# GNN and MoE layer: the gathered table of normed rows as plain fp32 instead of three bf16 parts

## The reference

```
xn  = layernorm(x)
agg = segment_sum(xn[src], dst) / max(degree, 1)
z   = concat([xn, agg]) @ gnn_weight            # 512 x 256
x1  = x + z / norm(z) + gnn_bias
xl  = layernorm(x1)
expert, gate = argmax and max of softmax(xl @ gate_w + gate_b)   # 8 experts
y   = w2[e] @ relu(w1[e] @ xl + b1[e]) + b2[e]  # 256 -> 1024 -> 256, capacity 977 a expert
out = x1 + y * gate                             # dropped tokens: y is of weight 0
```

## Time and profile before

| | us |
|---|---|
| median of 3 runs | 1463.89 (1462.98 to 1465.42) |
| the profiled execution | 1461.04, its span 1459.3 |
| mean granted TensorE clock | 0.94 |

### The profile page before, as it was taken

How to read it: one execution, slowest core, us unless ns; L and a number is a source line. 1 busy time by engine, 2 the same in 40 slices (tenths; PEclk the granted TensorE clock), 3 DMA queues, 4 the chain that set the end, 5 groups by cost and what they waited for, 6 DMA issues and landing times.

```text
span 1459.3 us, 33188 instructions
## 1 busy us (share of the span) xinstructions
PE 1101.7 (75%) x6813; PEld 797.5 (55%) x6814; DVE 874.6 (60%) x3786; ACT 495.6 (34%) x1397; POOL 923.8 (63%) x946
## 2 busy tenths in 40 slices
PE   0105667668888888888889889888888888876885
PEld 0004445446666666666666666666666666654553
DVE  2973545446666676666667666666756675654443
ACT  1651111223333333333333333333333333343442
POOL 3446676757777777777777777777776777600101
PEclk9998777879999999999999999999999999998998
DMA  7257888865565656566565655656564656411111
GB/s 210 89 185 211 299 267 287 286 213 162 163 179 165 183 162 186 168 174 179 155 176 149 181 159 168 168 160 174 149 179 131 176 152 174 127 38 43 37 48 35
DMA packets 126952, 238.78 MB, mean 164 GB/s; under 512 B 21453, under 2 KB 85250, under 8 KB 126932
## 3 DMA queue, kind: packets, MB, share of 16 engines
q0 software_dynamic: 55904, 160.90, 38.6%
q1 hardware_dynamic: 71028, 77.69, 16.9%
HBM read 207.46 MB, written 39.29 MB: 169 GB/s over the span
## 4 chain that ended last, share of the span: by engine, by line
DVE 25%; DVEq 20%; PE 20%; issue 17%; DMA 14%; ACT 3%; SPq 1%; ACTq 1%; POOL 1%; POOLq 0%
PE ps_q L726 7%; DVEq L1300 5%; PE ps_h L793 4%; DMA ring<-parts_d,idx 4%; PE ps_a L784 4%; DVE sel L1049 3%; DVEq L1120 3%; DMA b_b<-in_L_ffn_b 2%; DMA parts_d<-w_sb 2%; DVEq L903 2%; DVE row L1163 2%; DMA out<-ys,node_i 2%; DMA w_sb<-in_x 2%; DVE row L1167 1%; DVE acc L1058 1%
## 5 line engine op out<-in xcount | busy, mean ns | idle before, releaser
L476 POOL DMA_INDIRECT ring<-parts_d,idx x784 | 768.2, 980 | 278.5 <-issue 184.4
L726 PE MATMUL ps_q<-ring,sel 128*128 128x256 bf16 x2928 | 474.6, 287 | 165.8 <-DVE sel L1049 90.4
L726 PEld LDWEIGHTS ps_q<-ring,sel 128*128 128x128 bf16 x2928 | 255.1, 102 | 325.0 <-issue 205.4
L1049 DVE SCALAR_TENSOR_TENSOR sel<-lane,block,dst_t 128x512 bf16<-128x512 bf16 x245 | 184.1, 751 | 121.2 <-PE ps_q L732 63.2
L812 PE MATMUL ps_b<-w_sb,hid_t 128*128 x864 | 231.0, 397 | 23.7 <-ACT hid_t L646 23.7
L793 PE MATMUL ps_h<-w_sb,hid_t 128*128 x432 | 211.1, 615 | 5.7 <-ACT hid_t L625 5.7
L1058 DVE TENSOR_TENSOR acc<-acc,ps_q 128x257 f32 x245 | 103.2, 421 | 164.0 <-ACT cat L600 68.1
L812 PEld LDWEIGHTS ps_b<-w_sb,hid_t 128*128 128x128 f32 x864 | 150.1, 190 | 48.3 <-issue 33.7
L732 PE MATMUL ps_q<-ones_bf,sel 128*128 128x1 bf16 x976 | 167.3, 171 | 0.0
L784 PE MATMUL ps_a<-gw_sb,cat_t 128*128 128x256 f32 x416 | 127.6, 435 | 0.9 <-ACT cat_t L622 0.9
L646 ACT ACTIVATE hid_t<-ps_t,b_t 128x128 f32<-128x128 f32 x432 | 117.6, 383 | 30.5 <-PE ps_t L801 30.5
(11 more groups left out here) (189 smaller groups left out, 1307.2 us busy)
## 6 DMA issues: line engine op xcount, KB each, us to landing
w_sb<-in_L_ffn_w SPq DMA_DIRECT2D x32, 512.0 KB
ring<-parts_d,idx POOLq DMA_INDIRECT x784
disp_d<-ys SPq DMA_DIRECT2D x8, 1040.0 KB, 12.9
parts_d<-w_sb SPq DMA_DIRECT2D x6, 1344.0 KB, 5.1
xs<-disp_d SPq DMA_DIRECT2D x55, 130.0 KB, 3.2
ys<-disp_d SPq DMA_DIRECT2D x55, 130.0 KB
b_b<-in_L_ffn_b SPq DMA_DIRECT2D x55, 128.0 KB
xb<-in_x SPq DMA_DIRECT2D x51, 128.0 KB
```

What stands on the lines that cost most here:

```text
L476: pool.indirect_dma_start(ring[:, (k % 2) * TQ + j, :], None, parts_d[:, :], bass.IndirectOffsetOnAxis(ap=idx[:, k * TQ + j:k * TQ + j + 1 ...
L726: mm = pe.matmul(ps[:, 0:D], sel[:, s, j, :], ring[:, (k % 2) * TQ + j, part * D:(part + 1) * D], start=(j == 0 and part == 0), stop=(j == ...
L1049: dve.scalar_tensor_tensor(out=sel[:, s, :, :], in0=lane[:, :].rearrange("p (j m) -> p j m", j=1).to_broadcast((P, TQ, P)), scalar=block0[ ...
```

## The change

The table in HBM is `xn_d`, one fp32 row of 256 a node (1024 bytes). x has room for all seven groups in w1's memory; it is normalised in place, six of seven blocks on ACT and one on DVE, and each group is stored when both are done. The parts, their copies and their slots are gone. The statistics of two groups share one reciprocal step, with EPS added in it. The ring holds 257 fp32 a slot, the last of them 1, written once by POOL; the selection is fp32. A tile is one fp32 matmul of 257 columns, the last tile of a visit one of 256 and one of a single column. The first x group comes in two pieces. The second half of the edge lists is loaded as 96 rows by SP and one by POOL, the last x and table rows as 96 and 10. DVE clears `acc` in one instruction at the start, ahead of its statistics, and takes the edge reductions between the first two groups (by a minimum on the four results instead of a masked copy of the list). ACT's copies of the transposed edge lists come before its first group, into and out of two PSUM tiles in turn. The filler of the dispatch buffer comes from `hid`, not `ys`, so the first chunk loads are issued before trip 0; ACT waits for the fills before trip 8. w2 is loaded together with w1 at the start of a trip. POOL clears only the tail of the last group and makes the identity earlier.

```diff
@@ -25,9 +25,10 @@
 FULLQ = E_EDGES // QE
 TAIL = E_EDGES - FULLQ * QE
 PAD_DST = 16383
-NPART = 3
 XG = 7
-XA = 5
+XA = 6
+LASTA = LAST // 16 * 16
+ROWSA = (FULLQ - QH) // 16 * 16
 NG = NB // XG
...
-    parts_d = nc.dram_tensor("parts_d", (N, NPART * D), BF16, kind="Internal").ap()
+    xn_d = nc.dram_tensor("xn_d", (N, D), FP32, kind="Internal").ap()
...
-        ring = sb("ring", [P, 2 * TQ, NPART * D], BF16)
+        ring = sb("ring", [P, 2 * TQ, AW], FP32)
...
-        sel = sb("sel", [P, 2, TQ, P], BF16)
+        sel = sb("sel", [P, 2, TQ, P], FP32)
...
+            def store_xn(g):
+                blocks = XG if g < NG - 1 else XG - 1
+                sp.dma_start(xn_d[ds(g * (XG * P), blocks * P), :].rearrange("(b p) d -> p b d", p=P),
+                             xin[g][:, 0:blocks * D].rearrange("p (b d) -> p b d", d=D)).then_inc(xn_out, 16)
+                if g == NG - 1:
+                    for lo, hi in ((0, LASTA), (LASTA, LAST)):
+                        sp.dma_start(xn_d[(NB - 1) * P + lo:(NB - 1) * P + hi, :],
+                                     xin[g][lo:hi, (XG - 1) * D:XG * D]).then_inc(xn_out, 16)
 
...
-                sp.dma_start(staged[0:FULLQ - QH, QE:2 * QE],
-                             dram[QH * QE:FULLQ * QE].rearrange("(p e) -> p e", e=QE)).then_inc(stage_in, 16)
+                sp.dma_start(staged[0:ROWSA, QE:2 * QE],
+                             dram[QH * QE:(QH + ROWSA) * QE].rearrange("(p e) -> p e", e=QE)).then_inc(stage_in, 16)
...
+            sp.wait_ge(filler, 1)
+            sp.dma_start(disp_d[EX * SLOTS:DISP_ROWS, :], hid[:, 0:ROW]).then_inc(x1_out, 16)
             for g in range(NG):
-                s = g % 2
-                sp.wait_ge(low_done, g + 1)
-                sp.wait_ge(mid_copied, g + 1)
...
@@ -344,6 +340,7 @@
                 if weights:
                     fill_block(t)
                     load_weights(t, 0)
+                    load_weights(t, 1)
                 if node:
...
-                if weights:
-                    load_weights(t, 1)
...
+            load_xs(C0)
+            load_ys(C0 - 1)
             with sp.Fori(0, C0) as t:
                 trip(t, chunk=False, weights=True)
-            sp.wait_ge(fill_out, 16 * C0)
-            load_xs(C0)
-            load_ys(C0 - 1)
...
+                pool.dma_start(staged[ROWSA:ROWSA + 1, QE:2 * QE],
+                               dram[(QH + ROWSA) * QE:FULLQ * QE].rearrange("(p e) -> p e", p=1)).then_inc(tail_in, 16)
...
-            AC = NB * AW // NG
-            for g in range(NG):
-                pool.memset(acc[:, g * AC:(g + 1) * AC], 0.0)
...
-                pool.tensor_tensor(
-                    out=parts[s][:, :].rearrange("p (b k d) -> p b k d", k=NPART, d=D)[:, :, 2, :],
...
-            pool.wait_ge(parts_out[0], 16 * (NG // 2 + 2))
-            pool.wait_ge(parts_out[1], 16 * (NG // 2))
+            pool.wait_ge(xn_out, 16 * (NG + 2))
...
-                    ring[:, (k % 2) * TQ + j, :], None, parts_d[:, :],
+                    ring[:, (k % 2) * TQ + j, 0:D], None, xn_d[:, :],
...
-                act.wait_ge(rstd_ready, g + 1)
-                if g >= 2:
-                    act.wait_ge(r1_ready, g - 1)
+                act.wait_ge(rstd_ready, g // 2 + 1)
...
-                    last = act.activation(xn[s][:, b * D:(b + 1) * D], xin[g][:, b * D:(b + 1) * D], ACT.Identity,
+                    last = act.activation(xin[g][:, b * D:(b + 1) * D], xin[g][:, b * D:(b + 1) * D], ACT.Identity,
...
-                act.activation(parts_view(g)[:, :, 0, :], top_half(xn[s]), ACT.Copy).then_inc(hi_copied, 1)
-                    mid_copy(g - 1)
...
-            mid_copy(NG - 1)
+                if g % 2 and g + 1 < NG:
+                    rstd_start(g + 1, min(2, NG - g - 1))
...
-                    for part in range(NPART):
-                        mm = pe.matmul(ps[:, 0:D], sel[:, s, j, :],
-                                       ring[:, (k % 2) * TQ + j, part * D:(part + 1) * D],
-                                       start=(j == 0 and part == 0), stop=(j == TQ - 1 and part == NPART - 1),
-                                       skip_group_check=True)
+                    width = AW if j < TQ - 1 else D
+                    mm = pe.matmul(ps[:, 0:width], sel[:, s, j, :], ring[:, (k % 2) * TQ + j, 0:width],
+                                   start=(j == 0), stop=(j == TQ - 1), skip_group_check=True)
                     if final:
                         mm.then_inc(ring_free, 1)
-                    mm = pe.matmul(ps[:, D:AW], sel[:, s, j, :], ones_bf[:, :], start=False,
-                                   stop=(j == TQ - 1), skip_group_check=True)
                     if j == TQ - 1:
+                        mm = pe.matmul(ps[:, D:AW], sel[:, s, j, :], ring[:, (k % 2) * TQ + j, D:AW],
+                                       start=False, stop=True, skip_group_check=True)
...
+            def normal(g):
                 for b in range(XA, XG):
                     c = g * XG + b
-                    mm = dve.tensor_scalar(xn[s][:, b * D:(b + 1) * D], xin[g][:, b * D:(b + 1) * D],
-                                           mv1[:, o + 2 * b:o + 2 * b + 1], rstd1[:, c:c + 1],
-                                           ALU.subtract, ALU.mult)
-                mm.then_inc(xn_dve, 1)
-                dve.drain()
-
-            def rest(g):
-                s = g % 2
-                dve.wait_ge(xn_act, g + 1)
-                if g >= 2:
-                    dve.wait_ge(mid_copied, g - 1)
-                    dve.wait_ge(low_done, g - 1)
-                dve.tensor_tensor(r1[s][:, :], xn[s][:, :],
-                                  xn[s][:, :].bitcast(BF16).rearrange("p (d t) -> p d t", t=2)[:, :, 1],
-                                  ALU.subtract).then_inc(r1_ready, 1)
-
+                    xn = dve.tensor_scalar(xin[g][:, b * D:(b + 1) * D], xin[g][:, b * D:(b + 1) * D],
+                                           mv1[:, 2 * c:2 * c + 1], rstd1[:, c:c + 1], ALU.subtract, ALU.mult)
+                xn.then_inc(xn_dve, 1)
+
+            dve.memset(dst_i[ROWSA:QH, QE:2 * QE], PAD_DST)
+            dve.memset(src_i[ROWSA:QH, QE:2 * QE], 0).then_inc(stage_clear, 1)
+            dve.memset(acc[:, :], 0.0)
             stats(0)
+            edge_lists()
             stats(1)
+            rstds(0, 2)
             for g in range(NG):
-                rstds(g)
-                if g:
-                    rest(g - 1)
+                normal(g)
                 if g + 2 < NG:
                     stats(g + 2)
-                if g == 1:
-                    edge_lists()
-                if g == 4:
+                if g % 2 and g + 1 < NG:
+                    rstds(g + 1, min(2, NG - g - 1))
+                if g == 0:
                     quad_table()
-            rest(NG - 1)
+            dve.drain()
```

More of the change, by code:

```diff
@@ L128, in gnn_moe_layer @@
         XW = XG * D
[L129 to L136, removed]
+        xin = [carve(w1_flat, g * XW, XW) for g in range(NG)]
+        at = NG * XW
+        bn1 = carve(w1_flat, at, XG * 6)
+        mv1 = carve(w1_flat, at + 64, NG * XG * 2)
+        nt1 = carve(w1_flat, at + 192, NG * XG)
+        ln1 = carve(w1_flat, at + 256, NG * XG)
+        b1_r = w1_flat[0:EX * JF, at + 320:at + 320 + P]
+        at = 0
         dst_i = carve(w2_flat, at, 2 * QE).bitcast(I32)
@@ L414, in _ @@
             pool.memset(ones[:, :], 1.0)
+            pool.memset(eps_t[:, :], EPS)
+            pool.memset(ring[:, :, D:AW], 1.0).then_inc(pool_step, 1)
+            pool.wait_ge(pool_step, 1)
+            pool.affine_select(out=ident[:, :], in_=ident[:, :], compare_op=ALU.not_equal, fill=1.0,
+                               base=0, pattern=[[-1, P]], channel_multiplier=1)
+            pool.affine_select(out=tri[:, :], in_=tri[:, :], compare_op=ALU.is_ge, fill=0.0,
+                               base=0, pattern=[[1, P]], channel_multiplier=-1).then_inc(consts, 1)
             pool.memset(seen[:, :], 0.0)
@@ L533, in _, with rsqrt_start @@
         def _(act):
-            def rsqrt_start(to, of, tmp):
-                act.activation(tmp, of, ACT.Ln)
+            def rsqrt_start(to, of, tmp, plus=0.0):
+                act.activation(tmp, of, ACT.Ln, bias=plus)
                 act.drain()
@@ L546, in rstd_start @@
                             ).then_inc(ln1_ready, 1)
-            def parts_view(g):
-                return parts[g % 2][:, :].rearrange("p (b k d) -> p b k d", k=NPART, d=D)
-            def top_half(f32):
-                return f32[:, :].bitcast(BF16).rearrange("p (b d t) -> p b d t", d=D, t=2)[:, :, :, 1]
-            def mid_copy(g):
-                act.wait_ge(r1_ready, g + 1)
-                act.activation(parts_view(g)[:, :, 1, :], top_half(r1[g % 2]), ACT.Copy).then_inc(mid_copied, 1)
@@ L659, in _ @@
                 trip(t, chunk=False)
+            act.wait_ge(fill_out, 16 * C0)
             with act.Fori(C0, TRIPS) as t:
@@ L686, in _ @@
```

(8 more changed lines are left out.)

168 lines of the change are left out of this document (64 added, 104 removed).

## The result

| | before | after |
|---|---|---|
| median of 4 runs, us | 1463.43 (1457.35 to 1465.42) | 1418.93 (1417.98 to 1421.57) |
| the profiled execution, its span | 1461.04, 1459.3 | 1421.57, 1419.8 |
| mean granted clock | 0.940 | 0.968 |

A forecast was written before the change was run, and what follows sets the result against it. DVE sets the pace, with a stretch of PE without slack before the crossing selection. Front -48, trips 0 to 8 -16, trips 9 to 48 +39 make -25 on 1461.0: 1436 us (median 1439), range 1420 to 1460, wider 1400 to 1482.

The forecast's parts named there:

- front: Work until the first visit: first matmul at 67 instead of 115 us, -48, between -38 and -55.
- trips 0 to 8: Trips loading weights, through trip 8: -16 us, between 0 and -30, from -5, -8 and -3.
- trips 9 to 48: Bulk of the main loop: PE's longer tiles cost +1.1 a trip, +44, less 5 given back, +39 us.
- its own case: The prediction's main case: 1420 to 1460 us, a trip costing 0.7 to 1.5 more, chance 0.57.
- The row counts: Front transfers of 97 rows split into 96: if they stayed slow, DVE would wait from 16 until 27, front -38.
- POOL's floor of 21.3: Trips 1 to 7 can't go below POOL's 16 x 1.25 + 1.3 us; they were to gain 8 together.
- the sum of +1.05: Growth of PE's tight stretch before the crossing selection, with DVE waiting for it: 24.25 to 24.3 us a trip.
- two tiles with half a linear layer and one with the up layer: Start of PE's tight stretch: tile growth paid back by the passes behind, only the first costs 0.08 us.
- the up layer and PE's own register load behind it: same: In PE's tight stretch, after the counts: no change in time.
- Given back: Trips 9 to 48 lost 13 us to late gathers and clock dips; 5 of it was expected back.
- rival 3: Clock holds because PE idles less: 13 us back instead of 5, 6 more early, 1425 us; chance 0.10.
- Rivals 1 and 2: PE's growth all exposed, 2.2 a trip, 1483 us, chance 0.17; or all hidden, 1395 us, chance 0.13.

The follow-up runs named there:

- e1: Changed kernel with the front's transfers in 97 and 106 rows again: 0.971 of the kernel before's time, first selection at 75.46 us, 7.2 later.
- e2: Kernel before with only its 97-row transfers split into 96 and 1, 106-row ones into 96 and 10: 0.990, first selection at 94.33 instead of 111.65.
- e5: Changed kernel with SP holding each trip's fill and weight transfers until DVE has made the one-hot rows: 0.987 of the kernel before's time.
- e10: Changed kernel with PE's load of eight registers moved from behind the counts to behind the down layer's second step: 0.968 of the kernel before's time.
- e9: Changed kernel with all tiles as one 257-column matmul, no narrow matmuls, one ring slot released later: 0.957 of the kernel before's time, on a slower chip.
- e4: Changed kernel with acc cleared by POOL in 49 pieces instead of by DVE: 0.962 of the kernel before's time, slower chip; first selection at 75.19.
- e8: Changed kernel with acc cleared by ACT instead of DVE: 0.958 of the kernel before's time, on a slower chip; first selection at 61.65.
- f2: Changed kernel with ACT clearing acc early, all tiles 257 columns wide and PE's register load moved to the fourth quad: 1417.38 us, 0.967 of the kernel before's time.
- e7: Changed kernel with bf16 selection and only the upper 16 bits of gathered rows in the matmul, one pass a tile: 0.966 of the kernel before's time.

## Why the prediction was right, and where it was off

On the profiled execution it said 1436, and 1421.6 came: front +4.8, trips 0 to 8 +8.5, trips 9 to 48 -28.8, tail +1.0. The sign and the order of the terms held; the sizes of trips 0 to 8 and 9 to 48 did not, and the first two misses hide nearly half of the third, which is luck. The trip grew by 0.56, below the 0.7 to 1.5 of its own case, and the median of 1418.9 lies just under that case's 1420: the number fell in the wider range of 1400 to 1482, not in the narrow one.

**Front: right.** At the first matmul it gave 45.8 for 48 (69.2, 67 predicted); the other 2.6 of the +4.8 lie between that matmul and the mark, beside the stretched register load. The clear took 10.55 (11 taken), the waits for ACT's last step 2.76 (3), and the tables started at 54.1 (51), since the clear began only at 4.8 where the sum had 0.5. The row counts were called, at 10 us; e1 gives 7.2. The Trainium skill's rule for them ("DMA: Bandwidth & Descriptors", "Why a DMA increments its semaphore by 16 and not by 1"), a split over the largest count up to 16 that divides the outer size, agrees in sign in both directions: 7.2 us in e1, 17.3 in e2. No row here shows how many engines took part.

**Trips 0 to 8: half.** Trip 0 gave 4.2 (5 predicted), trip 8 3.1 (3), trips 1 to 7 0.2 instead of 8. What held them was not POOL's floor of 21.3 but DVE's chain: 23.7 to 23.8 in trips 2, 3 and 5, where PE waited for no gather. In it DVE's two register loads take 3.3 to 4.6 and 0.9 to 1.1 instead of 1.87 and 0.30; trip 7, where they are at 1.87 and 0.30, took 21.94. Before, the small one was at 0.30 and the large one at 2.0 to 4.7 (mean 3.2; 3.5 after), so some 0.9 a trip came back here. Three of the chain's steps in the changed kernel, two loads in trips that fill weights and one in a later trip:

```profile
93.80 4.61 DVEq L1245
167.77 3.37 DVEq L1245
...
287.83 1.91 DVEq L1245
```
e5 shows that the stretched load follows SP's issuing of the fill and the weights.

**Trips 9 to 48: the mechanism held, its size was halved.** PE's stretch has no gap from the second quad's selection to the crossing one, as said (the visit that ends it is the third quad's, which the prediction calls the second's), but it grew by 0.44. The step that failed is the sum of +1.05:
- "two tiles with half a linear layer and one with the up layer": +0.06 (4.76 to 4.82) for +0.08;
- the narrow fp32 matmul has a pitch of 0.14, not 0.22 to 0.28: the last tile of the second quad +0.10 for +0.24, that of the third +0.22 for +0.32;
- first tile of the next quad and the counts: +0.15, as said;
- "the up layer and PE's own register load behind it: same": -0.27. The load starts on PE's sequencer 0.05 ahead of the up layer's first pass now and 0.22 behind it before, so the 0.28 that PE stood behind it before (the row below) fell to 0.01;
- the two tiles in front of transposes, with the transposes: +0.13 (631.92 to 632.76, now 609.01 to 609.98) and +0.05 for +0.13 each.

```profile
631.92 0.50 PE L726 MATMUL ps_q<-ring,sel 128*128 128x256 bf16 x3 [0.28 <-issue]
```

The crossing selection follows the stretch 0.07 faster: the first two steps of the trip grew by 0.38. A second way to that selection is as long within 0.1. From the third quad's selection to the end of the second quad's last tile it grew by 0.14, by the next tile's 0.52 for 0.37 another 0.15, and DVE's row work from L1077 to the crossing selection takes 4.51 (4.44 before). So shortening PE's stretch alone wins little: e10 takes 0.27 out behind the counts and wins 0.03; e9 takes out two narrow matmuls, one of them ahead of the counts and so on both ways, and wins about 0.08. The other 0.18 of the period is in the last step, 0.16 of it between DVE's add and its selection (0.92, now 1.08). It is no PE time: e9 keeps it, and e4, e8 and f2, with the clear off DVE, have 0.97. What makes it is open.

**Given back:** 5 were taken for late gathers and clock dips. Over 39 periods the excess over the quiet trip fell from 13.0 to 3.7, and the last trip with quads, which is shorter than a quiet one, took 2.3 less: 11.6, so 39 times 0.56 came down to +10.1. In size that is the 13 of rival 3, given 0.10. That the clock alone brought it is not shown. Before, one excess of 2.2 stands beside a clock of 0.91 and no late gather, but the trip behind it kept 23.3 at 0.93 (rows below), and seven others kept 23.2 at 0.94. Another 10.3 were in trips 40 to 42, 46 and 47, where the crossing quad moves: there PE waited 7.3 us for gathers and the clock was 0.88 to 0.98. In e10 trips 40, 41, 46 and 47 still lose 5.2 with the clock at 1.00. And rival 3's further 6 in the early trips did not come, though their clock rose from 0.79 to 0.86.

```profile
365.70:391.10 25.40, 21.85 (x134) 15.96 (x134) 15.64 (x69) 8.41 (x25) 18.27 (x19) 0.91 0.57 163
391.10:414.40 23.30, 21.05 (x132) 15.50 (x133) 15.27 (x70) 8.13 (x25) 17.44 (x19) 0.93 0.60 173
```

The clock itself did what rival 3 said: with PE busy 851 of 927 us it was 1.00, in e7, with 683 of 929, it was 0.85. The rule behind it, activity releases the throttled clock (the Trainium skill, "TensorE: Matmul & The Clock Gate", "What's actually happening"), agrees from both sides.

Rivals 1 and 2 fell: 0.56 a trip is neither 2.2 nor 0. The selection stayed at 0.752, the gather's issue at 0.95, the tile's pitch is 0.43 as said. The POOL gap above 0.30 showed: one of 1.23 a trip, for DVE's slot.

## What to carry to other kernels

A narrow or short matmul costs what its neighbours let it: price it by its pitch in the new order, and ask of a sequencer's own load where it will start, not only how long it is. When two ways into one wait are equal within 0.1 us, shortening one is worth 0.1 at most; look for the second before counting a gain for every trip. Read a gain in a front together with the trips behind it: f2's front was 7.5 us shorter and its first nine trips 5.9 longer.

## What the runs showed that was not expected

- While POOL clears memory, a small DVE operation may stand for as long as POOL has clears queued: 12.64 us (e4), 1.80 beside one clear before.
- A load of eight registers from SBUF takes 1.87 us on DVE and 1.97 on PE, and up to 5.20 and 4.54 while SP issues transfers (e5 moves the delay from one engine to the other).
- Taking some 70% of a tile's PE time away (e7) made a quiet trip 0.12 us longer, with the clock at 0.85 instead of 1.00.
